# Routing front end: a second value product with gamma, rows written by VectorE, 24 selections on GpSimd

## What is computed

```python
x = x + xattn(layernorm(x), ctx, ctx, mask, gamma, beta)
x = x + ffn(layernorm(x), w_gate, w_gate_up, w_down)

def xattn(q, k, v, mask, gamma, beta):
    attn = softmax(where(mask == 0, -9e15, q @ k.T / sqrt(256)))
    a = attn @ v
    return (a - mean(a)) * rsqrt(var(a) + 1e-5) * gamma + beta

def ffn(x, w_gate, w_gate_up, w_down):        # 8 experts, each token goes to the best 2
    p = softmax(x @ w_gate); keep the 2 largest of each token, divide by their sum
    g, u = split(x @ w_gate_up[e]); y_e = (silu(g) * u) @ w_down[e]
    return sum over e of p[e] * y_e
```

## Time and profile before

| what | us |
|---|---|
| median of 3 runs | 468.27 |
| lowest and highest | 466.82, 468.73 |
| profiled execution, its own time | 468.64 |
| its span | 466.8 |

### The profile page before, as it was taken

How to read it: one execution, slowest core, us unless ns; L and a number is a source line. 1 busy time by engine, 2 the same in 40 slices (tenths; PEclk the granted TensorE clock), 3 DMA queues, 4 the chain that set the end, 5 groups by cost and what they waited for, 6 DMA issues and landing times.

```text
span 466.8 us, 10462 instructions
## 1 busy us (share of the span) xinstructions
PE 432.4 (93%) x2316; PEld 352.2 (75%) x2317; DVE 315.3 (68%) x802; ACT 222.0 (48%) x477; POOL 192.1 (41%) x207
## 2 busy tenths in 40 slices
PE   5999568899999999999999999999999999999980
PEld 3987234678888888888888888888888888888870
DVE  3478998787587567867776468767776487745530
ACT  2396492555455344636534345636534364434330
POOL 4156503445354435533454335543454435533211
PEclk8599789999999999999999999999999999999996
DMA  8617512345254414542552114542552133211121
GB/s 238 213 67 227 184 48 63 99 135 156 72 123 123 115 23 113 124 124 68 134 139 35 32 23 113 124 124 68 140 131 39 28 70 110 34 35 23 13 22 11
DMA packets 28649, 43.91 MB, mean 94 GB/s; under 512 B 2827, under 2 KB 22264, under 8 KB 28632
## 3 DMA queue, kind: packets, MB, share of 16 engines
q1 hardware_dynamic: 19274, 31.94, 22.0%
q0 software_dynamic: 7520, 10.39, 13.5%
q10 hardware_dynamic: 1838, 1.39, 1.2%
HBM read 34.07 MB, written 9.64 MB: 94 GB/s over the span
## 4 chain that ended last, share of the span: by engine, by line
PE 80%; DVE 7%; DMA 4%; issue 4%; POOL 2%; DVEq 1%; SPq 0%; POOLq 0%
PE bank L1316 45%; PE bank L1336 15%; PE bank L1338 8%; PE bank L1326 7%; DVE token_sel L704 2%; PE bank L1300 2%; DMA x_sb<-in_x 1%; PE bank L1164 1%; DMA tok<-rows_d,gather_i 1%; DVE scaled L660 1%; DMA out<-y_sb,out_i 1%; PE bank L1150 1%; DMA tok<-rows_d,gather 1%; PE bank L1120 1%; POOL x_sb L484 1%
## 5 line engine op out<-in xcount | busy, mean ns | idle before, releaser
L1316 PE MATMUL bank<-w,tokT_hi 128*128 (+1 forms) x624 | 173.7, 400 | 3.5 <-issue 1.3
L1062 ACT ACTIVATE gated<-bank,row_rstd 128x512 f32<-128x512 f32 x78 | 53.6, 688 | 182.0 <-PE bank L1316 181.9
L1316 PEld LDWEIGHTS bank<-w,tokT_hi 128*128 128x128 f32 x624 | 112.2, 188 | 28.6 <-issue 6.7
L1336 PE MATMUL bank<-w,aT_hi 128*128 (+1 forms) x312 | 118.5, 414 | 1.1 <-DVE y_sb L877 1.1
L856 DVE SCALAR_TENSOR_TENSOR act<-bank,row_rstd,gated 128x512 f32<-128x512 f32 x78 | 58.5, 749 | 82.4 <-ACT gated L1062 82.4
L555 POOL DMA_INDIRECT out<-y_sb,out_i x39 | 61.8, 1586 | 97.8 <-DVE y_sb L877 97.8
L1316 PE MATMUL bank<-w,tokT_lo 128*128 (+1 forms) x312 | 97.2, 393 | 0.0
L1338 PE MATMUL bank<-w,aT_lo 128*128 (+1 forms) x312 | 87.2, 280 | 0.0
L542 POOL TENSOR_TENSOR tok<-tok,beta_b 128x256 f32<-128x256 f32 x38 | 28.6, 751 | 108.3 <-DMA tok<-rows_d,gather_i 108.3
L1316 PEld LDWEIGHTS bank<-w,tokT_lo 128*128 128x128 f32 x312 | 58.6, 188 | 13.0
L1336 PEld LDWEIGHTS bank<-w,aT_hi 128*128 128x128 f32 x312 | 58.7, 188 | 11.5 <-issue 1.3
(11 more groups left out here) (170 smaller groups left out, 413.9 us busy)
## 6 DMA issues: line engine op xcount, KB each, us to landing
raw<-in_L_ffn_w_gate_up SPq DMA_DIRECT2D x32, 512.0 KB, 3.9
raw<-in_L_ffn_w_down SPq DMA_DIRECT2D x16, 512.0 KB, 3.8
rows_d<-x_sb SPq DMA_DIRECT2D x8, 264.0 KB, 3.1
x_sb<-in_x SPq DMA_DIRECT2D x8, 256.0 KB, 7.0
out<-x_sb SPq DMA_DIRECT2D x8, 256.0 KB, 4.0
out<-y_sb,out_i POOLq DMA_INDIRECT x39, 3.9
tok<-rows_d,gather_i POOLq DMA_INDIRECT x38, 3.7
vals<-in_ctx ACTq DMA_DIRECT2D x1, 462.0 KB
```

What stands on the lines that cost most here:

```text
L1062: act_e.activation(gated[:, h, :], ps_g[h][:, :], ACT.Silu, scale=row_rstd[:, s:s + 1]).then_inc(gated_set, 1)
L1316: ins = pe.matmul(ps[:, :], tokens_[:, s, k, :], w.rearrange("p a g d -> p (a g) d"), start=(k == 0 and tokens_ is tokT_hi and part == 0), ...
L1336: pe.matmul(ps_y[:, :], aT_hi[:, h, c, :], w.rearrange("p a t d -> p (a t d)"), start=(h == 0 and c == 0), stop=False, skip_group_check=True)
```

## The change

- The value product is split. `values` now makes 257 columns (variance and values). A second product, `values_gamma`, multiplies the same exponentials with `vals_g`: the centred context times gamma, and the gate columns. GpSimd makes `vals_g` (one 77x256 product per batch).
- VectorE computes the new row in one operation from PSUM: second product times scale, plus x, 264 wide. GpSimd's additions, the buffer `scaled`, `last_gates` and the separate addition of the last batch are gone.
- The loop handles the values of batch i-1 in iteration i (before, of batch i-2), so it has 9 iterations in place of 10.
- Row statistics are taken per batch and no longer per two batches; so are the inverse roots.
- GROUPS are 4, 4, 4, 2 and 2 tiles. The selections of the first three groups (24) are made by GpSimd, those of the last two by VectorE. ScalarE makes the place rows of tiles 0 to 14 in seven groups, VectorE those of tile 15.
- TensorE's first products wait for one constant in place of five; seven spins stand in place of four; the logits of batch 0 come before x of batch 1 is turned. SP loads `w_gate` first, and takes the later masks, the contexts from batch 4 and gamma over from ScalarE's queue. ScalarE runs one exponential early.
- On GpSimd `row_scale(0)` stands behind the second gather.

```diff
-    BY_ACT = NT - 2
+    BY_DVE = NT - 1
...
-    GROUPS = [range(0, 4), range(4, 8), range(8, NT - 2), range(NT - 2, NT)]
+    GROUPS = [range(0, 4), range(4, 8), range(8, 12), range(12, 14), range(14, 16)]
+    ACT_PLACES = [range(0, 2), range(2, 4), range(4, 6), range(6, 8), range(8, 12), range(12, 14), range(14, 15)]
+    POOL_GROUPS = 3
...
-        ps_att = [bank[i][:, 0:VAL] for i in (4, 5, 6) * 4 + (4, 5, 0, 1)]
+        ps_att = [bank[i][:, 0:VAL] for i in (4, 5)]
+        ps_attg = [bank[i][:, 0:ROW] for i in (6, 1)]
...
+            sp.dma_start(w_gate_sb[:], w_gate.rearrange("(k p) e -> p k e", p=P)).then_inc(wg_in, 16)
             load_x(0)
-            sp.dma_start(w_gate_sb[:], w_gate.rearrange("(k p) e -> p k e", p=P)).then_inc(wg_in, 16)
             sp.dma_start(cols_row[0:KD, :], gamma.rearrange("(k p) -> k p", p=P)).then_inc(cols_in, 16)
             sp.dma_start(cols_row[KD:2 * KD, :], beta.rearrange("(k p) -> k p", p=P)).then_inc(cols_in, 16)
-            for b in range(1, B):
+            load_x(1)
+            sp.dma_start(gamma_b[:], gamma.partition_broadcast(T)).then_inc(gamma_in, 16)
+            load_x(2)
+            sp.dma_start(cap[:, 4:NT, :].rearrange("p (b j) t -> p b (j t)", j=TPB).bitcast(I32), mask_t[:, 2:B, :]).then_inc(mask_in[1], 16)
+            load_x(3)
+            sp.dma_start(vals[:, 4:B, 1:D + 1], ctx_t[:, 4:B, :]).then_inc(ctx_in[2], 16)
+            for b in range(4, B):
...
-                if b < B - 1:
-                    sp.wait_ge(x1_set, b + 1)
-                else:
-                    sp.wait_ge(x1_last, 1)
-                if b == B - 1:
-                    sp.wait_ge(z_last, TPB)
+                sp.wait_ge(x1_set, TPB * (b + 1))
...
+            def x_rstd(b):
+
+                pool.wait_ge(var1, b + 1)
+                pool.tensor_tensor(rstd[:, tiles(b)], var_eps[:, tiles(b)], neg_half[:, 0:TPB], ALU.pow).then_inc(rstd1, 1)
...
-            def x1(b):
-
-                pool.wait_ge(scaled_set, TPB * (b + 1))
-                pool.wait_ge(x_gate_set, b + 1)
-                pool.tensor_tensor(x_sb[:, tiles(b), :], scaled[:, b % 2], x_sb[:, tiles(b), :], ALU.add).then_inc(x1_set, 1)
+            def values_gamma(b):
+
+                pool.wait_ge(gamma_in, 16)
+                pool.wait_ge(vals_set, b + 1)
+                pool.tensor_tensor(vals_g[:, b, 0:D], vals[:, b, 1:D + 1], gamma_b[:], ALU.mult).then_inc(vals_g_set, 1)
+
+            def select(i, g):
+
+                pool.wait_ge(parts_set, i + 1)
+                for t in g:
+                    for c in range(2):
+                        pool.tensor_scalar(token_sel[:, 2 * t + c, :], count_hi[:], hi[:, t, c:c + 1], number[:, t:t + 1],
+                                           ALU.is_equal, ALU.mult).then_inc(token_pool, 1)
...
-            for i in range(B // 2 - 1):
-                x_rstd(i)
-            for b in range(B):
-                scales(b)
-                if b < B - 1:
-                    x1(b)
-                if b == 0:
-                    x_rstd(B // 2 - 1)
+            x_rstd(0)
+            x_rstd(1)
+            values_gamma(0)
+            for i in range(B + 1):
+                if i + 2 < B:
+                    x_rstd(i + 2)
+                if i >= 1:
+                    scales(i - 1)
+                if i + 1 < B:
+                    values_gamma(i + 1)
+                if i >= 5:
+                    select((i - 5) // 2, range(2 * i - 10, 2 * i - 8))
+            select(2, GROUPS[2])
...
+            def x1(b):
+
                 dve.wait_ge(att_scale_set, b + 1)
                 dve.wait_ge(x_gate_set, b + 1)
                 for t in range(TPB * b, TPB * (b + 1)):
+                    dve.wait_ge(attg_ps, t + 1)
+                    dve.scalar_tensor_tensor(out=x_sb[:, t, :], in0=ps_attg[t % 2], scalar=att_scale[:, t:t + 1],
+                                             in1=x_sb[:, t, :], op0=ALU.mult, op1=ALU.add).then_inc(x1_set, 1)
...
+            def last_places():
+
+                dve.wait_ge(parts_set, len(GROUPS))
+                for t in range(BY_DVE, NT):
+                    for c in range(2):
+                        dve.tensor_scalar(place_sel(t)[:, c, :], neg_count[:], neg_lo[:, t, c:c + 1], None, ALU.is_equal).then_inc(last_place, 1)
...
+            x_stats(0)
             bans(0, 0, 2)
             dve.wait_ge(bias_ps, 1)
             dve.tensor_copy(bias_g[:], ps_bias).then_inc(bias_set, 1)
             masked_logits(0)
+            x_stats(1)
+            ctx_means(1, 2, 4)
             for i in range(B + 1):
+                if i + 2 < B:
+                    x_stats(i + 2)
+                if i == 3:
+                    split_low(dve, 0)
+                if i == 4:
+                    split_low(dve, 1)
+                if i == 8:
+                    slots(3, GROUPS[3])
                 if i + 1 < B:
                     masked_logits(i + 1)
+                if i == 0:
+                    ctx_means(2, 4, B)
+                    bans(1, 2, B)
+                if i >= 1:
+                    x1(i - 1)
+                if i == 3:
+                    dve.wait_ge(const, 15)
+                    choose(GROUPS[0])
+                if i == 4:
+                    slots(0, GROUPS[0])
                 if i == 5:
+                    choose(GROUPS[1])
                 if i == 6:
+                    slots(1, GROUPS[1])
+                    choose(GROUPS[2])
+                if i == 7:
                     split_low(dve, 2)
+                    slots(2, GROUPS[2])
+                    choose(GROUPS[3])
+            choose(GROUPS[4])
+            slots(4, GROUPS[4])
+            last_places()
+            select(4, GROUPS[4])
+            select(3, GROUPS[3])
...
+            def places(n):
+
+                g = ACT_PLACES[n]
+                act_e.wait_ge(parts_set, [i for i, h in enumerate(GROUPS) if g[0] in h][0] + 1)
...
+            centre(0)
+            centre(1)
+            copy_xT(0)
+            copy_ctxT(0)
+            copy_xT(1)
+            centre(2)
+            centre(3)
+            for i in range(B + 1):
+                if i >= 1:
+                    copy_pT(i - 1)
+                if i < B:
+                    exps(i)
+                if i < PAIRS:
+                    copy_ctxg(i)
+                if i >= 1:
+                    square(TPB * (i - 1))
+                    square(TPB * (i - 1) + 1)
+                if i + 2 < B:
+                    copy_xT(i + 2)
+                if i + 1 < PAIRS:
+                    copy_ctxT(i + 1)
+                if i < 2:
+                    centre(2 * i + 4)
+                    centre(2 * i + 5)
+                if 2 <= i < 5:
+                    split_high(act_e, i - 2)
+                if i == 6:
+                    places(0)
+                if i == 7:
+                    places(1)
+            places(2)
+            places(3)
+            places(4)
+            places(5)
+            places(6)
...
+                if b >= 1:
+                    pe.wait_ge(xT_set, b)
+                    spin(1, bank[0])
...
+                pe.wait_ge(vals_set, b + 1)
                 for j in range(TPB):
                     t = TPB * b + j
+                    if t >= 2:
+                        pe.wait_ge(squared, t - 1)
+                    pe.matmul(ps_att[j], probsT[:, b % 2, j, :], vals[:, b, :], start=True, stop=True).then_inc(att_ps, 1)
+
+            def values_gamma(b):
+
+                pe.wait_ge(vals_g_set, b + 1)
+                pe.wait_ge(ctxg_set, b // 2 + 1)
+                for j in range(TPB):
+                    t = TPB * b + j
+                    if t >= 2:
+                        pe.wait_ge(x1_set, t - 1)
+                    pe.matmul(ps_attg[j], probsT[:, b % 2, j, :], vals_g[:, b, :], start=True, stop=True).then_inc(attg_ps, 1)
...
+            pe.wait_ge(const, 1)
+            spin(7, bank[3])
             pe.wait_ge(wg_in, 16)
...
+            spin(1, bank[3])
+            turn_x(0)
             pe.wait_ge(cols_in, 32)
             pe.transpose(ps_cols, cols_row[:], ident[0:2 * KD, 0:2 * KD]).then_inc(cols_ps, 1)
             spin(2, bank[3])
...
+            turn_x(1)
+            spin(2, bank[3])
+            pe.wait_ge(const, 5)
+            for i in range(B + 1):
                 if i + 2 < B:
                     turn_x(i + 2)
+                if i >= 1:
+                    values(i - 1)
                 if i + 1 < B:
                     logits(i + 1)
+                if i + 1 < PAIRS:
+                    turn_ctx(i + 1)
+                if i >= 1:
+                    values_gamma(i - 1)
                 if i < B:
                     turn_probs(i)
+                if i + 1 < PAIRS:
+                    gate_ctx(i + 1)
+                if i == 4:
+                    ranks(0, GROUPS[0])
                 if i == 6:
                     ranks(1, GROUPS[1])
+                if i == 7:
+                    ranks(2, GROUPS[2])
+            ranks(3, GROUPS[3])
```

(52 more changed lines are left out.)

187 lines of the change are left out of this document (33 added, 154 removed).

## The result

| | us | |
|---|---|---|
| after, median of 4 | 479.23 | 478.77 to 479.44 |
| before, beside it, median of 4 | 467.87 | 466.82 to 468.73 |
| ratio | 1.0247 | [1.0218, 1.0276] |

The kernel became 2.5% slower, where 457 was predicted. The profiled execution took 479.4, its span 477.6. Run again later, the same kernel took 463.92 to 466.23 in eight executions, 471.27 in one and 479.62 to 480.12 in three: it runs in one of two ways, and the rest of this text needs both to be understood. I call them the execution near 480 (the profile after) and the one near 465 (profiled in that later run, span 463.5).

What follows compares the result with a forecast made beforehand. The front before the experts was taken as bound by TensorE's half clock, then VectorE's list: 4.4 (earlier start) + 7.7 (shorter list) = 12.1 off 468.64, 456.5; 457 for the median, own range 454 to 459, wider range 453.5 to 465.

Steps and rivals of the forecast that it cites:

- The loop's clock: TensorE's loop before the experts: full clock expected from about 5 us, an iteration 3.9 us, 4.7 while contexts are turned.
- the half clock as a rival: Head of the kernel: half clock until about 22.8 to 24, list starts at 24.3, 6.6 us off, 462; chance 0.17.
- The second product per tile is paid by the spins that go: TensorE's loop: removed spins offset the added gamma products, 3.9 us an iteration against 3.7 to 4.0 before.
- the slower rival: GpSimd selections above 1.35 us each eat all 12 us of gain; 473.3 at 1.5 us; chance 0.08.
- The start of the list: Third batch's row maximum, where VectorE's list begins: at 18.7 us instead of 23.17, 4.4 us less.
- VectorE's waits in the list: VectorE's idle time from the third maximum to the last selection or place row: 4.5 us, some 6 before.
- 16x(p-0.7): Loop scales wait behind four GpSimd selections of 0.8 to 1.2 us (p) in four iterations: 458 to 465; chance 0.10.
- The list's own work with sharing: VectorE's operations from the third maximum to its last selection or place row: 31.4 us, plus 2.4 for sharing with GpSimd.
- TensorE's end: Last spins and token products, about 4.1 us against VectorE's 3.5: TensorE ends 0.6 us later.
- The selection on GpSimd: One 128x128 compare and multiply on GpSimd: 0.45 us, its work per iteration 3.15 us, hidden in a period of 4.3.
- the early table load: ScalarE's exp table load at the head: gives 0.3 us of the earlier list start, at most 1.4 more.
- the rival of 460.5: Clock full in the head but down before the last token products: 4 us more, 460.5; chance 0.18.

Runs made afterwards that it cites:

- six forced waits: TensorE made to wait for the third 512 KB of weights in iteration 1: kernel after with four spin variants, kernel before with and without value-product spins; 472.76 to 483.05 us.
- the probe: Kernel after with eight spins in iteration 1, plus five 128x128 GpSimd instructions (compare and multiply, compare alone, add and multiply) between its first tasks: 469.46 us, one execution.
- the kernel before with the wait: Kernel before, its own spins kept, TensorE made to wait at the top of iteration 1 for the third 512 KB of weights: 472.76 us, one execution.

## Why the prediction was wrong, step by step

**The loop's clock: the step that failed.** "TensorE's loop body at 2.4 GHz", with full clock "from about 5 on and no 0.50 until 40", was the base of the list's start and of its length. In the profile after the clock fell at 7.3, rose at 17.5 and fell again at 21, within a gap of 1.11, and stayed at 0.50 until 48. Near 480 and near 465 are the same program, 14.2 us apart (479.4 and 465.2), and their gather indices 14.9: 5.7 up to the third maximum, 9.9 from there to the eighth, -0.7 behind it.

I had the half clock as a rival, but only up to 22.8 to 24, because the clock of before rose there. I read that rise as something that comes with time. It does not come with any fixed time: the new body had none for 27 us, twice. "The second product per tile is paid by the spins that go" was right for TensorE's time: with the clock up an iteration is 4.66, near the 4.7 that I had for the early ones. What it left out is that the loop might run at half clock, where an iteration is 9.0. The rival's 462 lacks the 9.9 us of the loop. No rival of mine had a fall that lasts through the loop, and the slower rival, a selection above 1.35, is not what happened (0.8). That the full clock failed is shown by the same program at 465 and at 480; that the edit made it fail, by taking spins out or putting products in, is likely (8 of 26 executions, none of 75 of the kernel before) but not shown: the old loop without its spins had none in ten.

TensorE: Matmul & The Clock Gate of the Trainium skill (Part 1, What's actually happening) says that "activity releases the throttle". The windows above do not agree with it as it stands: 27 us of TensorE's work without a gap did not release it. Nothing in my sum hung on that sentence, but a reader who goes by it would make the same mistake.

**What sets it off** is shown less well. Each of the six forced waits (4.4 to 7.0 us) was followed by half clock. In the profile after it was 1.11 us behind a stretch at half clock; near 465 the gap was 0.28 and there was no such stretch. With all selections on VectorE the clock fell at 17.7 where the last gaps were of 0.66 and 0.30, so a gap of 1 us isn't needed. The gap comes from ScalarE, whose centring of batches 4 and 5 stands ahead of the copy that the value products need, as I had it, and in the profile after waits 1.32 us for VectorE's context sum. What makes the head of one execution different from that of another stays open.

**The rest: 465.2 instead of 456.5.** With the clock up the gather indices stand at 66.51, 8.1 after the 58.4 that the sum implies. By its terms:
- The start of the list: 20.33 for 18.7, 1.6 more. Seven spins from 1.06 were as predicted; x of batch 0 was not, TensorE waits for it until 6.43 where I had 4.9.
- VectorE's waits in the list: 7.4 for 4.5, 2.9 more. The logits (L643) have 2.5 of them, since of the view's 4.7 the 2.21 of its first row ended at 20.33, where the list starts; 3.7 are at L658 on `att_scale`, 1.0 at `slot_c` L681 and 0.2 at L658 on TensorE. The prediction read the earlier trace rows in the same wrong way: of the 4.6 at L632 1.35 ended at 23.17, ahead of the list. The 3.7 on `att_scale` are GpSimd's: four selections of 0.8 stand ahead of each scale. I had this as a rival, 16x(p-0.7), which gives 1.6 at p=0.8; the run that gives GpSimd two at a time leaves 1.5 of the 3.7.
- The list's own work with sharing: 42.45 (20.33 to 62.78) less 7.4, 35.1 for 31.4+2.4, 1.3 more. The three splits have 0.5 of it, 1.30 each for 1.13; the rest was not traced. `beaten` is at 0.49, where it lasted 1.41; the additions on GpSimd beside which it was stretched are gone.
- TensorE's end: 3.7 from VectorE's last selection to the indices, 0.8 in before (69.71 to 70.51). That is 2.9 more, where I had 0.6. Again the selections: GpSimd's last twelve take 9.75 and end at 64.14.

1.6+2.9+1.3+2.3 is 8.1. The other 0.6 of the 8.7 between 456.5 and 465.2 lies behind the indices, with 390.2 in the expert stage for 389.3.

**The selection on GpSimd: a term mis-sized**, 0.45 for 0.78 to 0.94. I chose near the copy of 0.30 for its single stream; compare and multiply is not priced by streams, as the probe shows (0.44 for add and multiply, 0.80 with the compare). The GPSIMD Engine Reference of the Trainium skill (4.1, Engine selection) has one-input work at about line rate and two-input work at half of VectorE's speed; the measured selection with one tile of input is 3 times VectorE's 0.27, so the measurement decides. All of GpSimd's share in the selections is then worth little: the median of the executions near 465 is 465.0 with them and 465.8 without, on two chips.

**What held:** the expert stage within 0.1 in the profile after and 0.9 near 465; `x1` at 0.49 each and 0.89 a pair, as `scaled` in the earlier trace rows; the gamma values at 0.63 to 0.72 for 0.65; the early table load; and half clock late in the front (45 to 59 in the execution near 465), the rival of 460.5. What it cost there was not measured; TensorE waits for GpSimd's selections behind it.

## What to carry to other kernels

A forecast that counts on TensorE's full clock needs the half clock as a case of its own for every stretch that TensorE fills, here 9.9 us for the loop. A busy TensorE with a granted clock of 0.50 over many microseconds is a loss that no list of waits shows. When a kernel's gain hangs on the clock, measure many executions: four of four were near 480 here and then eight of twelve near 465; with eight spins ahead of the loop's first value products (1.7 us) none of 44 was near 480. One forced wait shows that the clock can stay down; one execution of it does not show how long a loop takes to come back. Before a difference is put down to an edit, look whether it begins ahead of the first instruction that the edit changes.

## What the runs showed that I had not expected

- A fully occupied TensorE at half clock for 27 us, in one body of products, twice; and the same products coming back from half clock after 3.4 us in one execution and after 10.2 in another.
- The row of the granted clock can be wrong. In the kernel before with the wait it reads 1.00 until 54, yet four logit products take nearly twice as long as later in the same profile. The third row here is the first value product, behind the return to full clock:

```profile
25.82 0.99 PE L1164 MATMUL bank<-ctxT,gated 128*128 128x85 f32 x4
...
28.68 0.60 PE L1150 MATMUL bank<-ident,x_sb 128*128 128x128 f32 x4
...
29.34 0.61 PE L1192 MATMUL bank<-vals,y_sb 77*128 77x265 f32 x2
...
30.94 0.57 PE L1164 MATMUL bank<-ctxT,gated 128*128 128x85 f32 x4
```

  It reads 1.00 through the head of the kernel before without spins, too, where the logits take 1.13. So the durations of a known product are the safer reading.
- On GpSimd a 128x128 compare is 0.59, compare and multiply 0.80, add and multiply 0.44.
- The best kernels found are those with the eight spins and 16 selections in portions of two: 465.11 and 464.61, 0.6% and 0.5% under before. The kernel after is as fast in its executions near 465 (465.0, 0.5% under before); what the others add is that none was near 480.
